# Window attention of a fused adaLN block: maxima subtracted on VectorE, one exponential per pair of heads, single-bank queries and keys, copies of turned weights on ScalarE, new orders

## What is computed

```python
def local_attention(q, k, v):              # per layer, 8 heads of 64
    bq = q.reshape(b, h, w, WINDOW, d) * QK_SCALE
    bk, bv = look_around(bk), look_around(bv)      # own window and the one before
    sim = jnp.einsum('bhwid,bhwjd->bhwij', bq, bk)
    sim = jnp.where(mask, -jnp.finfo(sim.dtype).max, sim)
    attn = jax.nn.softmax(sim, axis=-1)
    out = jnp.einsum('bhwij,bhwjd->bhwid', attn, bv)

def _layer(x, ...):                        # twice
    q, k, v = jnp.split(shift_token(x) @ wqkv, 3, axis=-1)
    q, k = l2norm(q) * qs, l2norm(k) * ksc
    q, k = rotary_xpos(q, k)
    x = x + local_attention(q, k, v) @ wo
    h = layernorm(shift_token(x)) @ w1 + b1
    a, g = jnp.split(h, 2, axis=-1)
    return x + (a * gelu(g)) @ w2 + b2
```

## Time and profile before

| what | value |
|---|---|
| median of three timed runs | 2146.88 us |
| span of the profiled execution | 2140.7 us |
| the profiled execution's own time beside the span | the page gives none but the span; the three timed runs lie 1.1 to 7.6 us above it |
| mean granted TensorE clock | 0.989 |
| busy: PE / DVE / ACT / POOL | 1949.1 / 1559.3 / 1607.3 / 862.1 us |
| one item in the steady state | 126.7 us |

### The profile page before, as it was taken

How to read it: one execution, slowest core, us unless ns; L and a number is a source line. 1 busy time by engine, 2 the same in 40 slices (tenths; PEclk the granted TensorE clock), 3 DMA queues, 4 the chain that set the end, 5 groups by cost and what they waited for, 6 DMA issues and landing times.

```text
span 2140.7 us, 56185 instructions
## 1 busy us (share of the span) xinstructions
PE 1949.1 (91%) x22308; PEld 1117.7 (52%) x22308; DVE 1559.3 (73%) x2671; ACT 1607.3 (75%) x3975; POOL 862.1 (40%) x826
## 2 busy tenths in 40 slices
PE   6789999999999999999999999999999999999987
PEld 3344545555454655545555554655545455554644
DVE  3476787877778777787877778687777877777753
ACT  1567878787887878777787887878688787877755
POOL 2043616245351624526163361625435162452522
PEclk8999999999999999999999999999999999999999
DMA  4110201213030120202112030120203012030100
GB/s 137 29 32 16 61 7 36 41 24 58 7 68 9 39 43 24 58 7 57 21 32 51 24 58 7 38 39 24 58 7 70 13 36 42 24 53 7 36 6 23
DMA packets 63110, 76.19 MB, mean 36 GB/s; under 512 B 10630, under 2 KB 57856, under 8 KB 60800
## 3 DMA queue, kind: packets, MB, share of 16 engines
q1 hardware_dynamic: 62852, 72.60, 16.1%
HBM read 9.14 MB, written 4.19 MB: 6 GB/s over the span
## 4 chain that ended last, share of the span: by engine, by line
PE 56%; ACT 23%; DVE 12%; issue 5%; SPq 2%; DMA 1%; POOL 1%; DVEq 0%; ACTq 0%; POOLq 0%
PE ps L430 10%; ACT pr L815 6%; PE ps L667 5%; PE ps L564 5%; ACT pr L777 5%; PE ps L594 4%; PE ps L595 4%; PE ps L604 4%; PE ps L658 3%; PE ps L449 3%; ACT pr L788 3%; DVE wm L1000 3%; PE ps L678 2%; PE ps L445 2%; PE ps L687 2%
## 5 line engine op out<-in xcount | busy, mean ns | idle before, releaser
L1091 POOL TENSOR_TENSOR pr<-pr 128x1024 f32<-128x1024 f32 x128 | 302.2, 2361 | 739.7 <-DVE pr L989 739.7
L815 ACT ACTIVATE pr<-ps,wb,inv 128x128 f32<-128x128 f32 x768 | 340.8, 481 | 24.6 <-DVE wb L1006 24.2
L777 ACT ACTIVATE pr<-ps 128x1024 f32<-128x1024 f32 x320 | 314.4, 1028 | 42.5 <-PE ps L449 42.0
L1108 POOL TENSOR_TENSOR pr<-pr,shares 128x512 f32<-128x512 f32 x192 | 199.9, 1048 | 314.0 <-DVE shares L1021 314.0
L947 DVE TENSOR_REDUCE nm<-ps 128x2 f32<-128x256 f32 (+2 forms) x384 | 314.5, 861 | 13.0 <-PE ps L449 11.9
L430 PE MATMUL ps<-cf,pr 128*128 128x128 f32 x1792 | 259.7, 282 | 31.1 <-POOL pr L1108 22.5
L430 PEld LDWEIGHTS ps<-cf,pr 128*128 128x128 f32 x1792 | 200.9, 142 | 124.4 <-issue 55.0
L982 DVE TENSOR_TENSOR pr<-ps,rot 128x1024 f32<-128x1024 f32 x128 | 156.2, 1221 | 120.1 <-ACT pr L788 97.7
L788 ACT ACTIVATE pr<-ps 128x1024 f32<-128x1024 f32 x128 | 131.2, 1025 | 104.6 <-PE ps L595 66.2
L445 PE MATMUL ps<-cb 64*64 64x256 bf16 (+1 forms) x2560 | 175.3, 263 | 30.1 <-ACT pr L777 14.4
L1014 DVE COPY pr<-ps 128x512 f32<-128x512 f32 x256 | 170.1, 679 | 15.2 <-PE ps L430 13.7
(11 more groups left out here) (158 smaller groups left out, 4040.0 us busy)
## 6 DMA issues: line engine op xcount, KB each, us to landing
pr<-V SPq DMA_DIRECT2D x32, 512.0 KB, 4.5
queries<-early SPq DMA_DIRECT2D x224, 64.0 KB
keys<-early SPq DMA_DIRECT2D x224, 64.0 KB
pr<-V SPq DMA_DIRECT2D x32, 384.0 KB, 6.6
xn<-in_L_attn_x SPq DMA_DIRECT2D x16, 256.0 KB, 4.5
out<-hT SPq DMA_DIRECT2D x16, 256.0 KB, 2.2
queries<-mT SPq DMA_DIRECT2D x128, 4.0 KB
Wqkv<-in_L_ffn_wqkv SPq DMA_DIRECT2D x1, 1536.0 KB
```

Source lines behind the costliest of these rows:

```text
L777: act.activation(dst, src, ACT.Exp, scale=SC1).then_inc(ex_r[s], 1)
L815: ins = act.activation(P2[s][2 * (p % 3) + r][:, o:o + P], bank[:, r * T + o:r * T + o + P], ACT.Exp, scale=inv[s][:, t, h:h + 1], bias=wb ...
L1091: pool.tensor_tensor(t1[s][t % 3], t1[s][t % 3], t2[s], ALU.add).then_inc(sum_r[s], 1)
L1108: pool.tensor_tensor(part, part, share, ALU.mult).then_inc(part_r[s], 1)
```

## The change

Six things are edited together.

1. The queries too are multiplied by their inverse norms, on POOL (`norm`, now two multiplications of 128x512). So the scores need no scale.
2. `wscore` on DVE: maxima as before, then one subtraction of 128x1024 from PSUM to SBUF. The score banks are free after it. The small product by the inverse norms goes.
3. `wexp`: one exponential of 128x1024 in place in SBUF for both heads, without row sums. `share` on DVE sums the rows (128x1024) and inverts 8 sums; on POOL it multiplies two heads, one after the other.
4. `pturn`: the turned weights are copied by ACT and no longer by DVE.
5. `qkv` and `rotate` are split in a half for the queries and one for the keys (`j`), each with one PSUM bank; the squares, cosine, sine and POOL additions are split with them. The sum of squares stays one instruction.
6. New `PLACES`, `TURNS` and `FIRST_BANKS`, with an order of its own for even and for odd items; `FILLS` is empty. `y` and the third weight buffer now lie in `scr`.

```diff
-            out += [("qkv", l, t), ("rotate", l, t), ("v", l, t)] * (t < NT) + [("norm", l, t - 1)] * (1 <= t <= NT)
+            out += [("qkv", l, t, 0), ("rotate", l, t, 0), ("qkv", l, t, 1), ("rotate", l, t, 1), ("v", l, t)] * (t < NT) + [("norm", l, t - 1)] * (1 <= t <= NT)
...
-            out += [("wscore", l, p), ("wexp", l, p, 0), ("share", l, p, 0), ("wexp", l, p, 1), ("share", l, p, 1)] * (p < NP2)
+            out += [("wscore", l, p), ("wexp", l, p), ("share", l, p)] * (p < NP2)
...
-    2318: 4, 2325: 1,
-}
+FILLS = {}
...
                     elif kind == "wexp":
+                        l, p = a
+                        act.wait_ge(*wd_r.at(b, NP2 * l + p + 1))
+                        act.activation(P2[s][p % 3], P2[s][p % 3], ACT.Exp).then_inc(we_r[s], 1)
+                    elif kind == "pturn":
                         l, p, r = a
                         n = NP2 * l + p
...
+                        if 2 * p + r >= 3:
+                            banks.wait(act, (b, "pv", l, (2 * p + r - 3) // 2))
+                        bank = banks.wait(act, (b, "pturn", l, p, r))
+                        act.activation(PT[s][:, (2 * n + r) % 3, :], bank, ACT.Copy).then_inc(pt_r[s], 1)
...
+                        low = wm2[s][:, 2 * p:2 * p + 2, :].rearrange("p r t -> p (r t)")
+                        dve.tensor_reduce(low, src.rearrange("p (j n) -> p j n", n=P), AX_X, ALU.max, negate=True).then_inc(wm_r[s], 1)
                         dve.wait_ge(*wm_r.at(b, n + 1))
...
+                        dve.tensor_tensor(P2[s][p % 3].rearrange("p (j n) -> p j n", n=P), src.rearrange("p (j n) -> p j n", n=P),
+                                          low.unsqueeze(2).broadcast_to([P, 2 * NT, P]), ALU.add).then_inc(wd_r[s], 1)
+                    elif kind == "share":
+                        l, p = a
+                        n = NP2 * l + p
+                        total = sums[s][:, 2 * p:2 * p + 2, :].rearrange("p r t -> p (r t)")
+                        dve.wait_ge(*we_r.at(b, n + 1))
...
+                        dve.tensor_reduce(total, P2[s][p % 3].rearrange("p (j n) -> p j n", n=P), AX_X, ALU.add).then_inc(sum_w[s], 1)
...
+                        dve.reciprocal(shares[s][:, 2 * p:2 * p + 2, :].rearrange("p r t -> p (r t)"), total).then_inc(share_r[s], 1)
...
-                        v = t1[s][t % 3][:, T:2 * T].rearrange("p (h d) -> p h d", d=D2)
-                        one = inv[s][:, t, H2:2 * H2].unsqueeze(2).broadcast_to([P, H2, D2])
-                        pool.tensor_tensor(v, v, one, ALU.mult).then_inc(rot_r[s], 1)
+                        for j in range(2):
+                            v = t1[s][t % 3][:, j * T:(j + 1) * T].rearrange("p (h d) -> p h d", d=D2)
+                            one = inv[s][:, t, j * H2:(j + 1) * H2].unsqueeze(2).broadcast_to([P, H2, D2])
+                            pool.tensor_tensor(v, v, one, ALU.mult).then_inc(rot_r[s], 1)
```

More of the change, by code:

```diff
@@ L77, in steps @@
     out += [("final",)]
-    cut = out.index(("qkv", DEPTH - 1, 0)) + 1
-    first = {("kheads", DEPTH - 1, 2): [("stats", 0)], ("kheads", DEPTH - 1, 3): [("plain", 0)],
-             ("wscore", DEPTH - 1, 0): [("load",)], ("wscore", DEPTH - 1, 1): [("proj", 0), ("proj", 1)]}
-    between = []
-    for last in out[cut:]:
-        between += [(1, last)] + [(0, name) for name in first.get(last, [])]
-    return between + [(0, name) for name in out[:cut]]
-PLACES = {
[8 rows of a table removed]
-    "ACT": [
[6 rows of a table removed]
-    "DVE": [
[5 rows of a table removed]
-    "POOL": [
-        0, 3, 5, 7, 9, 15, 13, 18, 24, 28, 30, 35, 37, 42, 44, 50, 52, 32, 33, 70, 122, 130, 127, 135, 133, 137,
-        139, 145, 143, 148, 155, 157, 160, 162, 167, 169, 175, 177],
-    "SP": [
-        25, 31, 40, 48, 32, 33, 158, 165, 173, 76, 82, 93, 106, 68, 153, 125],
+    return out
@@ new lines @@
+PLACES = {
+    "PE": (
+        [
[8 rows of a table added]
+        [
[8 rows of a table added]
+    ),
+    "ACT": (
+        [
[7 rows of a table added]
+        [
[7 rows of a table added]
+    ),
+    "DVE": (
+        [
[4 rows of a table added]
+        [
[4 rows of a table added]
+    ),
+    "POOL": (
+        [
+            551, 554, 559, 565, 197, 198, 200, 252, 260, 262, 269, 265, 267, 275, 271, 273, 283, 279, 281, 286, 293,
+            296, 301, 307, 1, 324, 326, 333, 329, 331, 339, 335, 337, 347, 343, 345, 350],
+        [
+            454, 456, 463, 459, 461, 469, 465, 467, 477, 473, 475, 480, 487, 490, 495, 501, 518, 520, 527, 523, 525,
+            533, 529, 531, 541, 537, 539, 544, 195, 551, 554, 559, 565, 197, 198, 200, 252],
+    ),
+    "SP": (
+        [
+            3, 4, 12, 18, 387, 29, 42, 61, 97, 161],
+        [
+            581, 255, 291, 355, 3, 4, 12, 18, 29, 42],
+    ),
@@ L141 @@
+    "SP": (
+        "01bd20b7b20b7b20b7b20b7b20b7b20b7b20b7bb"),
 }
 def merged(engine):
-    names = [steps()[i] for i in PLACES[engine]]
-    rest = [iter([(b, name) for k in range(B // S2 + 1) for back, name in names for b in [s + S2 * (k - back)] if 0 <= b < B])
-            for s in range(S2)]
+    names = steps()
+    rest = [iter([(b, names[i % len(names)]) for k in range(B // S2 + 4) for i in PLACES[engine][s]
+                  for b in [s + S2 * (k - i // len(names))] if 0 <= b < B]) for s in range(S2)]
@@ L286, in build @@
         hs = [sb(f"hs{s}", [P, T]) for s in range(S2)]
-        y = [sb(f"y{s}", [P, T]) for s in range(S2)]
         Q = [sb(f"Q{s}", [P, NP2 * T]) for s in range(S2)]
@@ L328, in build @@
         ctx2 = [a[:, 0:4 * T].rearrange("p (h n) -> p h n", n=T) for a in scr]
-        sums = [sb(f"sums{s}", [P, NT, H2]) for s in range(S2)]
-        shares = [sb(f"shares{s}", [P, NT, H2]) for s in range(S2)]
+        sums = [sb(f"sums{s}", [P, H2, NT]) for s in range(S2)]
+        shares = [sb(f"shares{s}", [P, H2, NT]) for s in range(S2)]
         hid = [a[:, 0:3 * T].rearrange("p (c n) -> p c n", n=T) for a in scr]
@@ L619, in step @@
                         n = NP2 * l + p
-                        bank, full = banks.take(pe, (b, "wscore", l, p), [we_r.at(b, 2 * n + 2)], 2)
+                        bank, full = banks.take(pe, (b, "wscore", l, p), [wd_r.at(b, n + 1)], 2)
                         if p == 0:
@@ L787, in step @@
                             act.wait_ge(*ss_r.at(b, n))
-                        act.activation(sqk[s], banks.wait(act, (b, "qkv", l, t)), ACT.Square).then_inc(sqk_r[s], 1)
+                        act.activation(sqk[s][:, j * T:(j + 1) * T], banks.wait(act, (b, "qkv", l, t, j)), ACT.Square).then_inc(sqk_r[s], 1)
                     elif kind == "v":
```

219 lines of the change are left out of this document (100 added, 119 removed), and 61 rows, old and new, of tables (FILLS, PLACES).

## The result

The changed kernel takes 2450.8 us (2442.8 to 2461.3) where the kernel before takes 2147.6 in the runs beside it: ratio 1.142, 95% interval 1.139 to 1.146. It is slower by 303 us; 2112 was forecast, with a range up to 2185.

The account below looks back on a forecast made before the run. PE was taken as the bound, busy 118.3 of 126.73 us an item. Terms of -0.8, -1.4 and -0.2 made -2.4 over 14.5 items, -35: span 2140.7 to 2106, plus 6.2 gives 2112 us, range 2030 to 2185.

Parts of the forecast that it names:

- stage 3: Window attention and feed-forward of layer 0 beside the next item's first attention, 55.50 us; forecast -0.8 us an item.
- ACT and DVE per item: Work of ScalarE and VectorE an item: ACT from 100.4 to about 93 us, DVE from 96.7 to 103.7.
- Table loads: On ACT, one more load an item, 1.28 us, or 2.7 by the skill's drain; 16 more in all.
- POOL's 8.3 us "priced at nothing while POOL has that room": Eight query products on POOL an item, 1.04 us each, in stages 2 and 4; priced at nothing, 1.04 each at worst.
- Stages 2 and 4: Next item's layer 0 projections, 27.23 us; layer 1 projections beside scores, 28.65: both PE's, forecast 0 and -1.4 us.
- Stage 1, 0: Layer 1's window attention beside the next item's join, out and scale, 15.35 us; forecast as long as before, 0.
- of the 4 us I charge 2 to 4: In stage 3, V copies queued on SP behind key transfers land 20 to 25 us in; charged 2 to 4 us.
- Rival (b): SP's queue decides: V copies land 4 to 8 us late, item +3 us, total +44, 2190 us; chance 0.18.
- The clock (c): Without fills PE's waits may halve its clock: 1.7 us an item, 25 in all, 2137 to 2145 us; chance 0.10.
- The ends and fills at 0: Ends, items 0 and 15 alone: 0. Removed fills in PE's waits, some five an item: nothing, apart from the clock.
- The bank split, -0.2: PSUM banks term: a score pair's two banks held 2.4 us instead of about 5.5; -0.2 us an item.

## Why the prediction was wrong

An item was to be 2.4 us shorter and is 20.0 longer. The work of ScalarE, VectorE and GpSimd came out within 2 us an item; TensorE is busy 125.6 us instead of 118.3 with the same products, at the lower clock. The step that failed is the price of waiting. The largest term is stage 3, forecast at -0.8, measured at +14.2: it charged the late copies of V and put the wait for the keys at nothing. Without the query and key transfers the changed kernel is 118 us faster. Next come the terms for new work, put at nothing where an engine had room by its busy share: scaling, maxima and sums give back 51 us of the changed kernel (on the old orders scaling alone cost 165), and 16 more with the transfers out. 120 of the 303 us stay open.

- **ACT and DVE per item**: forecast 93 and 103.7, measured 92.3 and 105.4; the exponential of 128x1024 forecast at 1.03, measured 1.056; the subtraction 1.224, the sum 1.207. Table loads: 16 more forecast, 121 for 93 counted, 28 more. The sum of work was right, and told nothing.
- **POOL's 8.3 us "priced at nothing while POOL has that room"** failed on the old orders most clearly. The room was read from a busy share, 20 of 27 us in stage 2. GpSimd's timeline of the kernel before has it working there without a gap from 1241.5 to 1261.0 (three of its rows stand above), on the tiles one after another: the room lay before and behind the chain, not in it. The part measured +165 us on the old orders, 10 us an item; 1.04 a stage had been its bound. 97 of them are the queue alone. On the new orders the same work gives back 29 when it is left out.
- **Stages 2 and 4 as TensorE's.** They were TensorE's only as long as GpSimd's 3.7 us a tile (2.36, 0.27 and 1.04) kept pace: 1.04 more a tile made stage 2 longer by 7.9. "0" for stage 2 measured +4.5 (part of it moved matmuls) and, with the old orders, +7.3; the -1.4 for stage 4 measured -0.9.
- **Stage 1, 0**: +0.1 in one kind of item, +4.4 in the other, where VectorE is busy 18.6 of 19.7 us. Of its 7 us more an item I had put 2.3 here in every item.
- **Stage 3, -0.8**: measured +14.2 in the mean. Two terms stand in it. The pair's chain: I let one engine's relief pay for the other's load, where VectorE was to be busy 47 of 55 us and passed by every pair four times; on the old orders this part cost +214 us above the scaling, on the new ones the maxima give back nothing and the sums 34. ScalarE's copies: counted as 9.7 us of its work, not as a place in its list; alone +222, with all else in 22.
- **SyncE's queue, "of the 4 us I charge 2 to 4"**: the landing was right, and so was the charge. The copies of V were forecast 20 to 25 us after the start of stage 3; their product started at 22.0 and 25.1, and the waits for them are 2.2 us in the mean and 3.4 at most. What failed is the wait in front of it. I counted the 14 key transfers only as what delays V, though TensorE's list, written out in the text, has the first maxima ahead of that product; they waited for the keys, up to 11.2 us. Moving the copies of V gained nothing; bringing the projection, and with it the transfers, forward gained 76. Rival (b) had the right queue, the wrong transfer and a third of its size.
- **The clock (c)**: the low clock came back in both kinds of item, as rival (c) had it: 0.83 to 0.92 in four of the eight stretches. The Trainium skill, "TensorE: Matmul & The Clock Gate", section "HAM oscillation — how this bites in real kernels", says that waits between bursts bring the lower clock back; the trace agrees here. The rival had 25 us for it. Fills that took away 187 us at half clock didn't move the time, so it isn't the main cause; its own share isn't shown.
- **The ends and fills at 0**: the fills were worth 14 us in the kernel before; the rest of the ends wasn't taken apart.
- **The bank split, -0.2**: measured -1.1 an item, the one part that gains. Alone it is the fastest kernel of this study, 2124.9.
- The load of a table: 1283 ns with the next instruction 0.02 us behind it also in the changed kernel; the drain that the Trainium skill ("ScalarE: Activation LUTs", section "What ACT_TABLE_LOAD costs") adds doesn't show behind it.

What stays open is 120 us on the new orders, left when the scaling, both passes and the transfers are out. In it are the subtraction, the single exponential for a pair, ScalarE's copies, the low clock, the wait for the output's store and the places of the other steps; they weren't parted, and giving the copies back to VectorE cost 168 there.

## What to carry to other kernels

An engine that is busy 70% of a stage may be the stage's pace: before work is added "in its room", look in its timeline for a stretch without gaps and ask whether the tiles pass through it in series. Price a moved operation by its place in the new engine's list, behind what it stands and who waits, and not by its duration: the same 0.6 us copy cost 222 us in one list and 22 in another, where it also left a fuller engine. Price a late transfer at its first reader in the list, not only at the reader you have in mind. Where a change brings both new work and new orders, each needs a price; run the new work on the old orders and the new orders without the work. And take the parts singly: one of the four here was a gain of 1%.
